# Gate and up projections of the second layer's FFN in three rounded matmuls instead of f32

## The reference

```python
x = L0_attn_x
xn = _layernorm(x)
x = x + attention(xn, W_K, W_Q, W_V, W_O) + binarised_linear(xn, weight, bias)
xn = _layernorm(x)
x = x + mamba2(xn, in_proj_w, conv_w, ...) + ffn(xn, gate_w, up_w, down_w, gate_s, up_s, down_s)

# ffn, 256 -> 704 -> 256:
g = einsum('th,ih->ti', xf, gate_w) * gate_s
u = einsum('th,ih->ti', xf, up_w) * up_s
out = einsum('ti,hi->th', silu(g) * u, down_w) * down_s
# mamba2, the parts that matter here: in_proj gives gate, x, B, C and dt;
# x, B, C pass a causal convolution of 4 taps and silu; dt = softplus(dt + dt_bias);
# dA = dt * A; its cumulative sums inside and across chunks weigh the state products.
```

## Time and profile before

| | |
|---|---|
| median of 3 runs | 2031.29 us |
| the profiled execution | 2029.76 us, its span 2028.0 us |
| mean granted TensorE clock | 0.987 of full speed |
| TensorE busy | 1951.2 us, 96% |
| VectorE busy | 1457.5 us, 72% |
| ScalarE busy | 1302.5 us, 64% |
| GpSimd busy | 834.3 us, 41% |

### The profile page before, as it was taken

How to read it: one execution, slowest core, us unless ns; L and a number is a source line. 1 busy time by engine, 2 the same in 40 slices (tenths; PEclk the granted TensorE clock), 3 DMA queues, 4 the chain that set the end, 5 groups by cost and what they waited for, 6 DMA issues and landing times.

```text
span 2028.0 us, 43010 instructions
## 1 busy us (share of the span) xinstructions
PE 1951.2 (96%) x12684; PEld 1588.1 (78%) x12684; DVE 1457.5 (72%) x2600; ACT 1302.5 (64%) x2978; POOL 834.3 (41%) x1000
## 2 busy tenths in 40 slices
PE   5999999999999999999989999999999999999998
PEld 4888678888788857888878885788878888588886
DVE  4775468888677457888857745788886773588886
ACT  3664269999555237888835523788884551488885
POOL 2120158888300005777620001577771000177776
PEclk8999999999999999999989999999999999999999
DMA  5330236566222113444412201344442220144442
GB/s 201 117 116 24 91 120 206 197 204 210 94 83 74 41 41 121 153 150 153 151 60 89 79 25 44 130 151 152 150 143 76 79 73 21 48 161 150 152 149 79
DMA packets 119115, 231.00 MB, mean 114 GB/s; under 512 B 10448, under 2 KB 48528, under 8 KB 118928
## 3 DMA queue, kind: packets, MB, share of 16 engines
q1 hardware_dynamic: 119056, 230.26, 34.5%
HBM read 194.05 MB, written 36.18 MB: 114 GB/s over the span
## 4 chain that ended last, share of the span: by engine, by line
PE 64%; issue 22%; ACT 9%; DVE 2%; POOL 2%; ACTq 1%; DMA 0%; POOLq 0%; DVEq 0%
PE bank L655 26%; PE bank L894 9%; PE bank L881 5%; PE bank L870 4%; PE bank L861 3%; PE bank L783 2%; PE both L655 2%; PE bank L775 2%; PE bank L755 2%; PE both L775 2%; PE bank L853 2%; ACT span_b L1158 2%; ACT place L1158 2%; ACT shared L1164 1%; PE bank L797 1%
## 5 line engine op out<-in xcount | busy, mean ns | idle before, releaser
L655 PE MATMUL bank<-xn_r,w_r 128*128 128x512 f32 x2304 | 631.6, 414 | 18.0 <-DVE place L1457 7.2
L655 PEld LDWEIGHTS bank<-xn_r,w_r 128*128 128x128 f32 x2304 | 425.1, 191 | 128.6 <-issue 41.9
L1315 DVE SCALAR_TENSOR_TENSOR conv_acc<-bank,conv_sb,conv_acc 128x511 f32<-128x511 f32 (+2 forms) x408 | 304.3, 746 | 51.0 <-ACT conv_acc L1076 17.3
L534 POOL TENSOR_TENSOR rstd<-var_eps,minus_half 128x4 f32<-128x4 f32 (+2 forms) x12 | 9.7, 809 | 664.0 <-DVE var_eps L1262 664.0
L1012 ACT ACTIVATE place_r<-bank 128x512 fp32r<-128x512 f32 (+1 forms) x320 | 158.1, 556 | 156.6 <-PE bank L655 128.7
L894 PE MATMUL bank<-wo_n,place 128*128 128x256 f32 x1024 | 255.1, 392 | 1.6 <-DVE place L1440 1.6
L1249 DVE TENSOR_TENSOR place_r<-bank,place_r 128x512 fp32r<-128x512 f32 (+1 forms) x320 | 186.7, 632 | 87.7 <-ACT place_r L1012 87.7
L555 POOL TENSOR_TENSOR shared<-shared,c_t 128x768 f32<-128x768 f32 x128 | 234.5, 1832 | 0.0
L894 PEld LDWEIGHTS bank<-wo_n,place 128*128 128x128 f32 x1024 | 184.0, 189 | 42.9 <-issue 21.2
L577 POOL TENSOR_TENSOR sumsq<-sumsq,place 128x512 f32<-128x512 f32 x128 | 163.5, 1277 | 110.6 <-ACT place L1065 110.6
L655 PE MATMUL bank<-place_r 128*128 128x512 f32 (+3 forms) x960 | 193.7, 342 | 9.4 <-DVE place_r L1249 6.8
(11 more groups left out here) (154 smaller groups left out, 3497.6 us busy)
## 6 DMA issues: line engine op xcount, KB each, us to landing
place_r<-cum_rows SPq DMA_DIRECT2D x128, 512.0 KB, 3.8
w_r<-pair_split SPq DMA_DIRECT2D x96, 512.0 KB, 3.7
w_r<-qkv_split SPq DMA_DIRECT2D x48, 512.0 KB, 4.0
pair_split<-w_r SPq DMA_DIRECT2D x32, 512.0 KB, 4.0
qkv_split<-w_r SPq DMA_DIRECT2D x16, 768.0 KB, 3.8
w_r<-qkv_split SPq DMA_DIRECT2D x48, 256.0 KB, 3.2
wo_n<-out_split SPq DMA_DIRECT2D x96, 128.0 KB, 3.5
raw<-in_w_pair SPq DMA_DIRECT2D x32, 256.0 KB, 3.8
```

The source lines that it names most:

```text
L655: ins = mm(out, lhsT=w(a), rhs=m(b), start=(start and i == 0), stop=(stop and i == 2), **kw)
L1315: stt(out=conv_acc[:, back:W], in0=src[:, 0:W - back], scalar=conv_sb[:, ch, TAPS - 1 - back:TAPS - back], in1=conv_acc[:, back:W], op0=AL ...
```

## The change

Gate and up are computed as `mm3` from `xn_r` and from weights in two parts. The high parts stay in SBUF (`gu_r`, in place of `gw_sb` and `uw_sb`). The raw weights are loaded into a stretch of `place`; in batch 0, after the last head, ScalarE makes the high parts and VectorE the low parts. The low parts lie in `place_r`: the gate's over q and k, the up projection's over the probabilities. SP saves both in HBM (`gu_kept`) in batch 0, and in each later batch fetches the first after the last scores and the second after the last head's values are summed.

Three moves in order come with it. TensorE waits for the low part of xn before tile 0 instead of before pair 0's x projection. ScalarE makes the high part of xn directly after xn is turned, and does Ln directly after Exp. VectorE makes dt_sb and da before the three taps of B's convolution.

```diff
+        gu_r = sb("gu_r", [P, 2, KT, F], F32R)
+        gu_low = [place_r[:, at:at + KT * F].rearrange("p (k f) -> p k f", k=KT) for at in (0, 8 * W)]
+        gu_raw = place[:, 5 * W:5 * W + 2 * KT * F].rearrange("p (m k f) -> p m k f", m=2, k=KT)
...
-                (gw_sb[:], gate_t), (uw_sb[:], up_t),
+                (gu_raw[:, 0, :, :], gate_t), (gu_raw[:, 1, :, :], up_t),
...
+            def gu_save(m):
+                sp.wait_ge(s_gu_low, m + 1)
+                sp.dma_start(gu_kept[m:m + 1, :, :]..., gu_low[m]...).then_inc(s_gu_saved, 16)
+            def gu_fetch(m):
+                sp.dma_start(gu_low[m]..., gu_kept[m:m + 1, :, :]...).then_inc(s_gu_fetched, 16)
...
                     pair_load(n, n)
+                for m in range(2):
+                    gu_save(m)
                 cum_save(0)
...
                     pair_fetch(n, n)
+                sp.wait_ge(s_scores_done, (b + 1) * NH * NT)
+                gu_fetch(0)
+                sp.wait_ge(s_z_done, (b + 1) * NH + 1)
+                gu_fetch(1)
                 if not last:
                     x_load(b + 1)
...
-                for w, bk, done in ((gw_sb, FFN_BANKS[f % 2][0], s_ffn_gate), (uw_sb, FFN_BANKS[f % 2][1], s_ffn_up)):
+                for g, done in ((0, s_ffn_gate), (1, s_ffn_up)):
+                    o = bank[FFN_BANKS[f % 2][g]][0:m, :]
                     for k in range(KT):
-                        ins = mm(bank[bk][0:m, :], lhsT=w[:, k, f * P:f * P + m], rhs=xn_t[:, k, :], ...)
+                        ins = mm3(o, lambda i: (gu_low[g][:, k, f * P:f * P + m] if i else gu_r[:, g, k, f * P:f * P + m]),
+                                  lambda i: xn_r[:, i, k, :], k == 0, k == KT - 1)
                     ins.then_inc(done, 1)
...
+                pe.wait_ge(s_xn_lo, (b * 2 + 2) * KT)
+                if first(b):
+                    pe.wait_ge(s_gu_low, 2)
+                else:
+                    pe.wait_ge(s_gu_fetched, b * 32)
                 ffn_hidden(b, 0)
...
+            def gu_split(m):                                   # ScalarE
+                A(gu_r[:, m, :, :], gu_raw[:, m, :, :], ACT.Copy).then_inc(s_gu_high, 1)
...
                 dve.wait_ge(s_late, 16 * N_LATE)               # VectorE
+                if first(b):
+                    for m in range(2):
+                        dve.wait_ge(s_gu_high, m + 1)
+                        tt(gu_low[m], gu_raw[:, m, :, :], gu_r[:, m, :, :].bitcast(F32), ALU.subtract).then_inc(s_gu_low, 1)
...
-                conv_taps(K, NPAIR, bank[0])
                 dve.wait_ge(s_dt_ln, b + 1)
...
                 ins.then_inc(s_da_ready, 1)
+                conv_taps(K, NPAIR, bank[0])
                 conv_end(K, b_t[:], bank[0])
```

## The result

| | before | after |
|---|---|---|
| median of the runs | 2031.82 us (2029.16 to 2035.76, 10 runs) | 2023.63 us (2021.43 to 2027.29, 10 runs) |
| ratio of the runs | | 0.9958, 95% interval 0.9948 to 0.9967 |
| profiled execution, its span | 2029.76, 2028.0 us | 2022.02, 2020.2 us |
| mean granted clock | 0.987 | 0.985 |

The kernel is faster by 0.42%, some 8.5 us. The forecast was 2021 us in a range of 2013 to 2028.

The account below looks back on a forecast made before the run. It took TensorE to bound the kernel, the second chain level with it at c_t. Gains of 1.17 us in batch 3 and 2.80 in each other make 9.6: 2029.76 to 2020.2, median 1.5 above, about 2021 us, range 2013 to 2028.

Parts of the forecast that it names:

- the second chain: ScalarE and VectorE beside TensorE: softplus of dt, convolutions of B and C, FFN gating; limits the gain to 9.6 of 19.0 us.
- The size of a tile: FFN gate and up on TensorE: 2.64 us a tile instead of 3.43; 24 tiles give a ceiling of 19.0 us.
- From c_t to the down projection: Stretch from the end of c_t to the down projection: 16.67 us instead of 18.90, 2.23 us less per batch.
- The wait before tile 5: TensorE, done with tiles 3 and 4, waits about 1 us for VectorE's tile 3 before tile 5.
- The reordering: Softplus ahead of B's taps: c_t 0.57 us earlier in batches 0 to 2, 1.06 us later in batch 3.
- Batch 3: the term that failed: Stage of batch 3: c_t 1.06 us later, 2.23 us less behind it, a gain of 1.17 us.
- rival 2: TensorE's clock falls in a new wait of one or two batches, up to 3.3 us each: 2023 to 2028; chance 0.21.
- Low parts of xn: cost nothing: ScalarE's copy and GpSimd's subtractions end before tile 0 needs them: no cost; without that cover 1.6 us at most.
- Rival 4: ScalarE's table load waits for Exp to drain: c_t 1.28 us later per batch, 5.1 us off the gain, 2026; chance 0.07.
- Rival 1: TensorE stays the bound and all 19.0 us come out, 2012; needs c_t by 1735.3 in batch 3; chance about 0.10.
- Rival 3: The clock falls before the B transpose in all four batches, 13.2 us against 9.6: slower, 2035; chance 0.06.
- The transfers and the splits of the weights: Saves and fetches never late, else up to 10 us a batch; batch 0's splits zero, 3.8 us once if uncovered.

Follow-up runs that it names:

- g1: Kernel before, plus seven f32 256-column filler matmuls in TensorE's 1.81 us wait and three in its 0.78 us wait ahead of the stage: 2029.3 us, ratio 0.9987.
- g2: f4 with tile 3 also ahead of the first x projection on TensorE: 2009.27 us, ratio 0.9889, the fastest version.
- f4: f3 with VectorE's product of tile 3 and its tanh ahead of the last two steps of the first x convolution: 2012.13 us, ratio 0.9899.
- e1: Changed kernel with the old order of softplus and B's taps restored on ScalarE and VectorE: 2026.08 us, ratio 0.9967.
- e2: Kernel before with only the new order of softplus and taps, gate and up still f32: 2031.46 us, ratio 1.0003.
- e3: Changed kernel without the low weight x high xn term in gate and up (two terms, not three): 2024.93 us, ratio 0.9968.
- e4: Changed kernel without the saves and fetches of the weights' low parts and the waits for them: 2022.03 us, ratio 0.9954.
- f2: Changed kernel with FFN tile 2 moved ahead of the B transpose on TensorE: 2024.63 us, ratio 0.9964.
- f1: Changed kernel with six and three rounded filler matmuls in TensorE's 1.81 and 0.78 us waits ahead of the stage: 2028.6 us, ratio 0.9982.
- g4: f1 plus eleven more filler matmuls in the wait for c_t ahead of the B transpose: 2022.32 us, ratio 0.9953.
- f3: Changed kernel with both edits, filler matmuls as in f1 and tile 2 moved as in f2: 2013.16 us, ratio 0.9910.

## Why the prediction was right, point by point

The mechanism held: the gain lies in the stage, it is capped by the second chain, and c_t to the down projection shrank by 2.4 to 2.8 us in every batch. That the sum came out near, 8.8 us in the stages for 9.6 forecast, is in part luck: batch 3 gave 1.1 us less and batch 2 0.6 less, batch 0 0.8 more. A slip in the last step counts too: 2020.2 + 1.5 is 2021.7 us, not 2021.

**The size of a tile was off.** The prediction took the spacing of rounded matmuls from the weight loads, "(2.62 - 0.19)/11 = 0.22 us apart". The matmuls themselves stand 0.2335 us apart: twelve in 1735.95 - 1733.07 = 2.88 us at the start of a stream, and in later tiles 1740.12 - 1737.32 = 2.80 for twelve. The ceiling was 24 x (3.43 - 2.80) = 15.1 us, not 19.0. That it was mostly a ceiling kept the error small; two tiles of each batch stand in the sum. The clean measure of it is the distance between two kernels in which TensorE is busy throughout at the full clock: 130.84 (g1) - 116.45 (g2) = 14.4 us over four stages.

**From c_t to the down projection: right.** c_t ends at 1731.27, and the down projection starts at 1747.67: 16.40 us, forecast 16.67. Inside, tile 2 took 0.24 more and tile 5 0.11 more, the two handovers that I put at 0.28 took 0.05 each, and the gate projection 1.37 instead of 1.50. The errors of the tiles (0.35 too little) and those of the handovers and the gate projection (0.59 too much) nearly cancel. The stretch that the second chain rules, from the x projection to the last step of tile 3, is 1742.64 - 1737.32 = 5.32 us, as forecast. The wait before tile 5 was 0.4 us and not 1, since two tiles took 5.6 us and not 5.28; f4 took it away.

**The reordering: right where the start is slow.** In batch 1 c_t ended 17.23 us after dt before and 16.67 after (c_t 738.07 + 0.69 and 734.63 + 0.69, VectorE before and after): 0.56 us earlier, forecast 0.57.

```profile
738.07 0.69 DVE L1324 SCALAR_TENSOR_TENSOR c_t<-bank,conv_acc 128x512 f32<-128x512 f32 x1 [0.67 <-ACT bank L1081]
...
734.63 0.69 DVE L1360 SCALAR_TENSOR_TENSOR c_t<-bank,conv_acc 128x512 f32<-128x512 f32 x1 [0.67 <-ACT bank L1112]
```

With 18.81 - 16.45 = 2.36 from c_t on, the stage gained 2.92 us, forecast 2.80. e1 gives the reordering about 2 us in all; the forecast had 3 x 0.57 - 1.06 = 0.65 net, since it counted on a loss in batch 3, where the slow start turned it into a gain.

**Batch 3: the term that failed.** The forecast had c_t 1.06 us later there, for a start at the full clock. In the changed kernel batch 3 started slow: 8.2 us to tile 0 instead of 5.3. c_t came 16.29 us after dt instead of 13.89, 2.40 later, and that took the whole 2.5 us gained behind it. The prediction had this as the last clause of rival 2 ("a shift in time may also give batch 3 a low clock at the dt matmuls"), with no price of its own. The basis was a rare stage: of 28 with both waits open it is the only one that started at the full clock. Part of that lies in which execution was profiled: in e2, whose TensorE order is that of the kernel before, batch 3 started partly slow too (7.0 us to tile 0, stage 34.49 us). But in all five kernels with the changed TensorE work and the two waits open (the changed one, e1, e3, e4, f2) batch 3 took 8.2 us there. What sets whether a batch starts slow behind the same two waits, no run here tells. And at a full clock the 1.06 was too small: c_t ends 13.8 to 13.9 us after dt in g1 and 15.8 to 15.9 in f1, 2.0 later. The rest is the 0.96 us that dt_tmp took longer, told below. A full clock would have left batch 3 a gain of some 0.5 us (32.25 us in g4 against 32.79), not 1.17.

**Batch 0 gave more than forecast, batch 2 less.** In batch 0 of the kernel before TensorE was not level with the second chain but 0.70 us late: c_t ended at 239.27, and the B transpose began at 239.97. So 2.84 us were there to be won behind c_t, and c_t came 0.73 earlier: 3.57 us, forecast 2.80. In batch 2 the clock rises midway through the start in both kernels (7.0 and 6.6 us to tile 0), and c_t came 0.19 us later instead of 0.57 earlier: 2.36 - 0.19 = 2.17. Together: 8.8 us measured in the stages, 9.6 forecast; 8.5 by the runs.

**"Low parts of xn: cost nothing" was wrong, and a low clock hid it.** GpSimd's subtraction now lies beside VectorE's first steps of softplus. Where the stage starts at the full clock, dt_tmp takes 1.38 us (f1, rows above) instead of 0.42, and 0.89 in batch 2 of the changed kernel; in batch 3, where GpSimd ended at 1718.56 and dt_tmp began at 1718.74, it took 0.43:

```profile
1716.06 2.50 POOL L614 TENSOR_TENSOR xn_r<-xn_t,xn_r 128x512 fp32r<-128x512 f32 x2 [2.86 <-ACT xn_r L1078]
...
1718.74 0.43 DVE L1429 SCALAR_TENSOR_TENSOR dt_tmp<-dt_raw 128x256 f32<-128x256 f32 x1
...
1220.25 2.49 POOL L614 TENSOR_TENSOR xn_r<-xn_t,xn_r 128x512 fp32r<-128x512 f32 x2 [2.84 <-ACT xn_r L1078]
...
1222.13 0.89 DVE L1429 SCALAR_TENSOR_TENSOR dt_tmp<-dt_raw 128x256 f32<-128x256 f32 x1
```

In each case the slowed instruction ends 0.3 us after GpSimd's (1220.25 + 2.49 = 1222.74 and 1223.02; in f1 1722.72 and 1723.00). The same holds over all the runs: GpSimd ends 3.6 us after the first dt matmul, and a dt_tmp that begins 2.5, 2.9 (e4, batch 0), 3.0 or 3.4 us (f2, batch 0) after it takes 1.38, 0.97, 0.89 or 0.44 us and ends 3.85 to 3.89 after it. In g1, with nothing on GpSimd beside it, one that begins at 2.4 takes 0.42. The Trainium skill (SBUF — State Buffer, "SBUF: two separate sides") has a lock for this: a VectorE instruction with two SBUF inputs and a GpSimd instruction that reads SBUF exclude one another for a whole instruction. By that rule dt_tmp, both of whose inputs lie in SBUF, waits until GpSimd is done, and that agrees with these ends to within 0.15 us: 0.28 us behind GpSimd is a little less than the 0.42 of a dt_tmp by itself. dt_raw, which reads a PSUM bank, took 0.42 beside the same GpSimd work in f1. I tried no kernel that moves the subtraction, so its price on the whole was not measured, and that the lock is the cause is argued from these ends; on c_t it is up to 0.96 us a batch, in the very batches in which TensorE waits for c_t.

**Rival 2** did not come true behind c_t in the changed kernel, where the wait is 0 to 1.17 us. Behind the B transpose its clock was 1.00 in all four batches. The clause on the dt matmuls of batch 3 did come true, as told above. Behind a wait the clock fell in e3 (2.1 to 3.0 us for c_t, three batches; 2.3 before tile 5, all four) and f1 (2.85, three of four), and g4 gives the price there: 1.3 to 1.6 us, not the 3.3 that I took from the slow start of a stage.

**Rival 4** (the table load waits for Exp to drain) fell: the load begins 0.02 us after Exp ends and Ln 0.01 us after the load, so there is no room for a drain. **Rival 1** fell with the chain: c_t did not come by 1735.3 - 1722.7 = 12.6 us after dt in any batch of the changed kernel. **Rival 3** fell with the clock of 1.00 behind c_t. **The transfers and the splits of the weights** cost nothing that shows, the first by e4, the second by VectorE's wait for the first attention output tile, which shrank from 7.23 us to 4.16 us around the two subtractions of 1.6 us each.

**What the change was worth beside its neighbour.** A full clock at the start of the stage would have shortened the stages of the kernel before by 8.6 us (g1), as much as the change did. The two don't add up by themselves: the changed kernel with a full clock at the start is slower (f1), until the order on TensorE gives it something to do (f3, f4, g2).

## What to carry to other kernels

Price a cheaper matmul by the distance of its own starts in a stream, and treat the saving as a ceiling: the stage ends with the second chain. When TensorE becomes cheaper than the chain beside it, a wait that opens may be paid twice, as those of 2 to 3 us in e3 and f1 were, once as a wait and once as slow matmuls behind it, so look for work to put into it. Edits of which one opens a wait and the other fills it should be tried together, since alone each may lose. And when work moves to a new place on GpSimd, look at what VectorE does beside it there.

## What the runs showed of the hardware that I had not expected

- Rounded 128x512 matmuls stand 0.2335 us apart in a stream of twelve, so that three of them, 0.70 us, save only 0.16 us against one f32 matmul (3.43/4 = 0.86 us). An f32 matmul over 256 columns took 3.19/7 = 0.46 us (g1), a little more than half of one over 512.
- Taking 22 us of TensorE work out of a kernel in which TensorE is busy for 96% of its span brought nothing (e3): in the profiled stages 15.0 us came back as waits and 11.2 as slower matmuls.
- Behind a wait of 2.85 us the granted clock was 0.65 on the mean of the next 4.7 us in batch 1 of f1, 0.71 and 0.64 in batches 2 and 3, and 1.00 in batch 0; with matmuls in that wait it was 1.00 in all four (g4).
- VectorE's dt_tmp took 1.38 us instead of 0.42 beside a GpSimd subtraction.
